# Weight preparation moved behind a norm in the attention, two roots split, and the router's folding moved one stage ahead, on one Trainium2 core

## The chip, the core and the metric

The kernel runs on one core of a Trainium2 chip. Its engines are TensorE (PE, with its weight loads as PEld), VectorE (DVE), ScalarE (ACT), GpSimd (POOL) and SyncE (SP, which only issues DMAs here). The metric is device microseconds of one execution of the whole program. Every engine runs its own list of instructions in order; they wait for one another by semaphores.

## What is computed

A two-layer network on x of 16 batches x 512 tokens x 128 features, float32. Each of four blocks is added to its input after a layer norm:

```
x = x + LN(attention(LN(x)))        # 16 heads of 8, keys and values through a latent of 32
x = x + LN(swiglu(LN(x)))           # hidden 384, weights are int32 times 1/127
x = x + LN(state_space_mlp(LN(x)))  # y = z + scan(rms(z)*scale1); y + gelu(rms(y)*scale2 @ w1 + b1) @ w2 + b2
x = x + LN(experts(LN(x)))          # spikes, router (tanh(cont@rW1+rb1)@rW2), top 2 of 8 experts
```

Here z is LN(x). `rms(z)` divides by sqrt(mean(z*z)+1e-6); a layer norm divides by sqrt(var+1e-5). The state space (16 states per feature) is computed as a convolution: matmuls with taps inside chunks of 128 tokens, and a carry between the four chunks of a batch.

## The kernel before

The program is a row of stages, each an `nc.Block()` with one hand-written list per engine and a barrier at its end: `attention` (tiles a_), `swiglu` (f_), `state_space` (m_), `mlp` (g_), `experts` (e_). X[:, b] is the running sum of batch b, Y[:, b+1] the output of the present block. Nothing schedules; order and semaphores are as written.

**Attention.** One body per batch t. In it 32 turns n: PE makes the scores of two heads against 128 keys (`score`, L629), DVE multiplies a part of them by the decay (`correct`, L775), ACT takes the exponential (L600), PE multiplies by the values (`weighted`, L636). Between the turns other batches' work is laid: POOL splits the next queries and keys into bf16 parts (`lower`), SP stores them to DRAM and reads them back spread by head (`spread_part`), and the norms of batch t-2 are finished: DVE writes `after_var` of t-2 at n = 11 (L179), POOL then inverts it and adds the normed output to X (`add_to`, L218 to L245), DVE waits for that at n = 24 (`wait_added`), takes the statistics of the sum (L165), and POOL inverts those (`next_norm.invert`, into xrstd). The last bodies are t = B-2 and B-1 (`ahead=False`), with B = 16.

After batch B-3's transfers SP also loads the integer weights of the swiglu into the buffers `parts` (L444, L446). POOL's `prepare_next_stage` waits for them, casts them to float (L513, 3 instructions) and normalises batch 0 for the next stage (L101, L104). PE, ACT and DVE need these only after the last body.

**swiglu's end.** `out_statistics`, `normalise` and `statistics` of the last batches run on DVE, then `moments` over all 16 batches at once gives xmean and var. `roots` holds var+1e-5 (for the layer norm) and var*(1+1e-6)+1e-11 (for u, the state space's input, which is normed twice); ACT takes the root of both in one instruction (L1569), DVE two reciprocals (L1712 xrstd, L1713 urstd). Then the barrier.

**state_space.** DVE makes the shifts -mean*rstd for u and for the layer norm (L1891). DVE and ACT then write u, 64 chunks of 128x128: DVE the 36 of batches 0 to 8 (L1895), ACT the 28 of batches 9 to 15 (L1833). PE starts when all of u is there (L1854). ACT then writes the layer norm of batches 0 to 11 into Y (L1839), POOL those of 12 to 15 (L1824, L1826). DVE makes the carries (L1903, L1907, L1909) and lays them in `blocks` (L1914) for PE (L1881), which in between makes the taps' products (L1870).

**mlp's start.** `squares_of` of batch 0, w1 times scale2 (L2078), the router's folding (`fold_router` on PE; `take_turned` and `take_folded` on DVE: s2c_W @ rW1 is put in the place of two matmuls), the first batch's norm (`rms_norm_first`, L2059, L2062), `squares_of` of batch 1, the copy of the transposed batch (`take_T`, L1429), then per batch four matmuls 128x512 (L2039), gelu on ACT, and 16 matmuls back (L2049).

## Time and profile before

| | |
|---|---|
| time, 3 runs | 1303.67 us median (1303.56 to 1304.56) |
| the profiled execution | 1303.26 us, span 1301.4 us, so 1.86 us lie around the span |
| mean granted TensorE clock | 0.962 of 2.4 GHz |
| busy share | PE 90%, DVE 73%, ACT 71%, POOL 50% |
| attention | about 0 to 618 us |
| swiglu | about 620 to 757 us |
| state_space | about 757 to 818 us |
| mlp | about 818 to 951 us |
| experts | to 1301.4 us |

The share of busy time is a mean over stages with different limits. The stage borders are places where all engines stop, so what sets the end differs from stretch to stretch; the rows below come from the stretches around the borders.

### The profile page before, as it was taken

The numbers are of one execution on the slowest core, as the hardware profiler recorded it, in microseconds if no ns is written. First come the engines' busy times: TensorE is split into PE (matmuls) and PEld (weight loads), VectorE is DVE, ScalarE is ACT, GpSimd is POOL, SyncE is SP. The second block draws the span as 40 slices with busy tenths as digits, with TensorE's granted clock in tenths as the row PEclk, the third lists the DMA queues.
The fourth block names the chain that finished last, engine by engine and source line by source line (L and its number), as shares of the span: only waits on it lengthen the run. The fifth ranks groups of instructions, "written<-read, shape, count | busy, mean of one in ns | idle before, by whom it ended". The sixth has DMA issues, their size and how long they took to land. (4 is left out here: it accounts for less than half of the span.)

```text
span 1301.4 us, 27430 instructions
## 1 busy us (share of the span) xinstructions
PE 1169.7 (90%) x7406; PEld 525.2 (40%) x7406; DVE 947.1 (73%) x2956; ACT 928.2 (71%) x1417; POOL 652.3 (50%) x1096
## 2 busy tenths in 40 slices
PE   4889999999999999948899839899979999999994
PEld 1222222322232322213566539577733444444432
DVE  5777777777777777637588877556566888888774
ACT  3979999999999999948556674355445666666664
POOL 5526656665655555334455540224233566666534
PEclk7989999999999999979899969899989999999998
DMA  5664555555555555600970003000000000000001
GB/s 157 143 123 97 106 114 103 110 107 112 108 107 105 108 106 110 118 15 1 228 237 19 1 2 130 1 0 0 1 0 1 10 9 16 16 8 17 9 17 33
DMA packets 71701, 87.97 MB, mean 68 GB/s; under 512 B 10369, under 2 KB 65191, under 8 KB 66023
## 3 DMA queue, kind: packets, MB, share of 16 engines
q1 hardware_dynamic: 69326, 85.81, 30.4%
q10 hardware_dynamic: 2296, 1.25, 0.4%
q8 instruction: 33, 0.54, 0.2%
q14 instruction: 46, 0.37, 0.1%
HBM read 63.84 MB, written 31.59 MB: 73 GB/s over the span
## 5 line engine op out<-in xcount | busy, mean ns | idle before, releaser
L600 ACT ACTIVATE a_probs<-a_S 128x1024 f32<-128x1024 f32 x512 | 492.3, 1035 | 61.0 <-DVE a_S L775 56.3
L775 DVE TENSOR_TENSOR a_S<-a_S,a_tables 128x256 f32<-128x256 f32 (+1 forms) x512 | 279.4, 561 | 129.3 <-PE a_S L629 124.4
L636 PE MATMUL a_O<-a_probs,a_V 128*32 128x512 f32 x2048 | 276.2, 612 | 1.7
L629 PE MATMUL a_S<-a_Qs,a_Ks 48*128 48x512 bf16 x1024 | 182.1, 388 | 34.8 <-ACT a_probs L600 29.3
L629 PEld LDWEIGHTS a_S<-a_Qs,a_Ks 48*128 48x128 bf16 x1024 | 43.6, 93 | 254.2 <-ACT a_probs L600 218.6
L2321 ACT ACTIVATE e_hid<-e_H 128x512 f32<-128x512 f32 x128 | 69.4, 594 | 48.1 <-PE e_H L2429 48.1
L2005 ACT ACTIVATE g_hid<-g_H,w_b 128x512 f32<-128x512 f32 x64 | 43.8, 687 | 57.2 <-PE g_H L2039 57.2
L481 POOL CAST w_first_parts<-a_whole 128x512 bf16<-128x512 f32 x15 | 9.1, 609 | 138.6 <-DVE a_whole L785 138.6
L2427 PE MATMUL e_H<-e_gated,w_We 64*128 64x512 f32 x256 | 73.2, 648 | 1.2 <-ACT e_hid L2321 1.2
L636 PEld LDWEIGHTS a_O<-a_probs,a_V 128*32 128x32 f32 x2048 | 40.4, 108 | 78.8 <-issue 64.8
L2438 PE MATMUL e_O<-e_hid,w_We 128*64 128x512 f32 x256 | 68.7, 609 | 0.4 <-ACT e_hid L2321 0.4
L2039 PE MATMUL g_H<-g_ynT,w_w 128*128 128x512 f32 x128 | 60.7, 619 | 1.6 <-DVE g_ynT L1429 1.6
L2049 PEld LDWEIGHTS g_OUT<-w_w,g_hid 128*128 128x128 f32 x512 | 59.7, 192 | 0.6
L2049 PE MATMUL g_OUT<-w_w,g_hid 128*128 128x128 f32 x512 | 59.7, 275 | 0.0
L2539 DVE TENSOR_TENSOR e_gated<-e_contT,e_G 128x512 f32<-128x512 f32 x64 | 44.0, 687 | 21.2 <-PE e_G L2419 19.7
L1555 ACT ACTIVATE f_gated<-f_G 128x512 f32<-128x512 f32 x48 | 28.6, 596 | 31.2 <-PE f_U L1592 31.2
L1603 PE MATMUL f_OUT<-w_wT,f_hid 128*128 128x128 f32 x384 | 46.5, 278 | 1.0 <-DVE XY L1669 1.0
L1603 PEld LDWEIGHTS f_OUT<-w_wT,f_hid 128*128 128x128 f32 x384 | 44.2, 192 | 5.5 <-DVE XY L1669 4.3
L652 PE MATMUL a_M<-ident,a_Osb 128*128 128x128 f32 x256 | 42.1, 287 | 4.6 <-DVE a_whole L785 3.8
L1638 DVE SCALAR_TENSOR_TENSOR f_hid<-f_U,f_gated 128x512 f32<-128x512 f32 x48 | 33.0, 690 | 14.6 <-ACT f_gated L1555 14.6
L218 POOL TENSOR_TENSOR g_power_rstd<-g_power_var,g_power_half 128x4 f32<-128x4 f32 (+1 forms) x15 | 15.1, 1007 | 56.2 <-DVE g_power_var L195 55.9
L652 PEld LDWEIGHTS a_M<-ident,a_Osb 128*128 128x128 f32 x256 | 27.1, 141 | 39.7 <-issue 26.4
(431 smaller groups left out, 2466.9 us busy)
## 6 DMA issues: line engine op xcount, KB each, us to landing
a_parts_dram<-a_parts SPq DMA_DIRECT2D x62, 192.0 KB, 5.7
a_Qs<-a_parts_dram SPq DMA_DIRECT2D x60, 192.0 KB
m_taps_by_step<-h_taps SPq DMA_DIRECT2D x8, 1024.0 KB, 13.6
m_taps<-m_taps_by_step SPq DMA_DIRECT2D x8, 1024.0 KB, 5.1
a_Qs<-a_parts_dram SPq DMA_DIRECT2D x60, 128.0 KB
a_parts_dram<-w_first_parts SPq DMA_DIRECT2D x32, 192.0 KB, 2.7
a_Ks<-a_parts_dram SPq DMA_DIRECT2D x30, 192.0 KB
a_Qs<-a_parts_dram SPq DMA_DIRECT2D x68, 64.0 KB
```

The costliest lines, as they stand in the source:

```text
L600: act.activation(probs[n % KEPT][:], S[n % RING][:], ACT.Exp).then_inc(exped, 1)
L629: mm = pe.matmul(S[n % RING][:, par, :], Ks[p][rows, pr, kb * P:(kb + 1) * P], Qs[p][Q_OF(kb)][rows, pr, :], start=True, stop=True)
L636: mm = pe.matmul(O[VC * j:VC * (j + 1), :], V[q][:, kb, HG * g + j, :], probs[(2 * m + j // 2) % KEPT][:, j % 2, :], start=(kb == 0), stop ...
L652: mm = pe.transpose(M[:, tile_of(core, c)], src[:, tile_of(core, c)], core.ident[:])
L775: v.tensor_tensor(s[:, :, where], s[:, :, where], wide, ALU.mult).then_inc(corrected, 1)
L1603: mm = pe.matmul(OUT[q].t[:, tile_of(core, c)], hid[q][:, m, tile_of(core, c)], wT[2][:, m, :], start=(m == 0), stop=(m == FC - 1))
L2039: pe.matmul(H[m][:], w1[:, tile_of(core, m)], ynT[p][:], start=True, stop=True).then_inc(h_full, 1)
L2049: mm = pe.matmul(o, hid[p][:, m, tile_of(core, c)], w2[:, m, :], start=False, stop=(m == FC - 1), skip_group_check=True)
L2321: HB[h].emptied(act.activation(hid[:, 2 * k + h], HB[h].t[:], ACT.Relu))
L2427: pe.matmul(HB[h].t[:], W.We1[half[h], k], gated[k % 2][half[h]], start=True, stop=False)
L2438: mm = pe.matmul(OB.t[h * M:(h + 1) * M], W.We2[:, 2 * k + h, :], hid[:, 2 * k + h, :], start=(k == 0 and h == 1), stop=(k == PAIRS - 1), ...
L2539: GB.emptied(v.tensor_tensor(gated[k % 2][:], contT[q][:], GB.t[:], ALU.mult))
```

## The change

Five edits.

1. In the attention POOL's `prepare_next_stage()` no longer stands at the head of body B-2 but at its end, behind `add_to` and `next_norm.invert` of batch B-4.
2. At swiglu's end the two roots have tensors of their own (xrstd is used in place): ACT takes u's root first, then the layer norm's; DVE there makes only the reciprocal of u's. The other reciprocal and its shift go into state_space, behind DVE's chunks of u. DVE now writes 38 chunks of u, ACT 26. ACT and POOL wait for the late shift (`UPPER`) before they write the layer norm.
3. The router's folding goes from mlp's start to swiglu's end: `fold_router` on PE behind the last `down`, into swiglu's PSUM tile G[0]; `take_turned`, `take_folded` and the cast of `select` (was DVE's L1086 in `shape_biases`) on ACT.
4. w1 times scale2 goes from DVE at mlp's start to POOL at the end of its list in state_space, as a `tensor_tensor` 128x512.
5. At mlp's start DVE takes the statistics of batch 1 between the variance of batch 0 and its norm, and the copy of the transposed batch 0 comes behind only the short rest of `squares_of` of batch 1.

```diff
@@ attention, POOL
             def body(t, p, first=False, ahead=True, more=True, fresh=True):
-                if isinstance(t, int) and t == B - 2:
-                    prepare_next_stage()
                 if not isinstance(t, int) or t >= 2:
                     out_norm.add_to(pool, t - 2, p)
                 if not ahead:
...
                     next_norm.invert(pool, t - 2, core.xrstd, p)
                     if not more:
                         next_norm.invert(pool, t - 1, core.xrstd, 1 - p)
+                    else:
+                        prepare_next_stage()
                     return
@@ Weights
+    def take_selection(self, act):
+        act.wait_ge(*self.experts)
+        act.activation(self.select.rearrange("p k m -> p (k m)"), self.table[:, 0:self.select.shape[1] * P], ACT.Copy).then_inc(self.shaped, 1)
+
-    def take_turned(self, v, ps):
-        v.wait_ge(self.folded, self.TURNED)
-        v.tensor_copy(self.s2cT, ps[0:self.s2cT.shape[0], 0:self.s2cT.shape[1]]).then_inc(self.folded, 1)
+    def take_turned(self, act, ps):
+        act.wait_ge(self.shaped, self.SELECTED)
+        act.wait_ge(self.folded, self.TURNED)
+        act.activation(self.s2cT, ps[0:self.s2cT.shape[0], 0:self.s2cT.shape[1]], ACT.Copy).then_inc(self.folded, 1)
@@ swiglu, ACT, PE, DVE
+            OUT[1].read(act, B // 2)
+            W.take_selection(act)
+            W.take_turned(act, G[0])
+            W.take_folded(act, G[0])
             act.wait_ge(steps, ROOTS)
-            act.activation(roots[:], roots[:], ACT.Sqrt).then_inc(rooted, 1)
+            act.activation(uroots[:], uroots[:], ACT.Sqrt).then_inc(rooted, 1)
+            act.activation(xroots, xroots, ACT.Sqrt).then_inc(rooted, 1)
...
             down(1, B // 2)
+            W.fold_router(core, pe, G[0])
...
             v.wait_ge(rooted, 2)
-            tick.mark(v.reciprocal(core.xrstd[:, 0:B], roots[:, 0]))
-            tick.step(v.reciprocal(core.urstd[:, 0:B], roots[:, 1]))
+            tick.step(v.reciprocal(core.urstd[:, 0:B], uroots[:]))
@@ state_space
-    ACT_U, ACT_BATCHES = 7, 12
+    DVE_CHUNKS, ACT_BATCHES = 38, 12
...
+            pool.wait_ge(dve_ready, UPPER)
             for b in range(ACT_BATCHES, B):
...
+            pool.wait_ge(*W.mlp)
+            pool.tensor_tensor(W.w1[:], W.w1[:], W.scale2[:].to_broadcast(list(W.w1.shape)), ALU.mult)
...
+            act.wait_ge(dve_ready, UPPER)
             act.preload_act_table(ACT.Exp)
...
+            shift_by(ushift, core.urstd)
+            for b, c in chunks[:DVE_CHUNKS]:
...
+            v.reciprocal(core.xrstd[:, 0:B], core.xrstd[:, 0:B]).then_inc(dve_ready, 1)
+            v.wait_ge(dve_ready, UPPER_ROOTS)
+            shift_by(shift, core.xrstd)
@@ mlp
-            W.fold_router(core, pe, folding)
-            pe.wait_ge(scaled, 1)
...
             power.squares_of(v, 0, Y[:, 1])
-            v.wait_ge(*W.mlp)
-            v.tensor_scalar(w1[:], w1[:], s2[:], None, ALU.mult).then_inc(scaled, 1)
-            W.take_turned(v, folding)
+            power.moments_of(v, 1, Y[:, 2], only_stats=True)
             rms_norm_first()
-            W.take_folded(v, folding)
-            power.squares_of(v, 1, Y[:, 2])
+            power.squares_of(v, 1)
             take_T(0, 0)
```

The order of POOL's list at body B-2 of the attention, before (line numbers of the changed kernel are one higher here; after_ and next_ are the two norms' tiles):

```order
L513 CAST a_whole<-w_first_parts 128x384
L513 CAST a_whole<-a_parts 128x384 x2
L101 TENSOR_TENSOR a_xn<-XY,xmean 128x512
L104 TENSOR_TENSOR a_xn<-a_xn,xrstd 128x512
L218 TENSOR_TENSOR after_rstd<-after_var,next_half 128x4
L220 TENSOR_TENSOR after_work<-after_rstd 128x4
L222 TENSOR_TENSOR after_work<-after_work,after_var 128x4
L224 TENSOR_TENSOR after_work<-next_three,after_work 128x4
L226 TENSOR_TENSOR after_rstd<-after_rstd,after_work 128x4
L241 TENSOR_TENSOR XY<-XY,after_neg 128x512
L243 TENSOR_TENSOR XY<-XY,after_rstd 128x512
L245 TENSOR_TENSOR XY<-XY 128x512
```

and in the changed kernel:

```order
L225 TENSOR_TENSOR after_work<-next_three,after_work 128x4
L227 TENSOR_TENSOR after_rstd<-after_rstd,after_work 128x4
L242 TENSOR_TENSOR XY<-XY,after_neg 128x512
L244 TENSOR_TENSOR XY<-XY,after_rstd 128x512
L246 TENSOR_TENSOR XY<-XY 128x512
L219 TENSOR_TENSOR xrstd<-next_var,next_half 128x4
L221 TENSOR_TENSOR next_work<-xrstd 128x4
L223 TENSOR_TENSOR next_work<-next_work,next_var 128x4
L225 TENSOR_TENSOR next_work<-next_three,next_work 128x4
L227 TENSOR_TENSOR xrstd<-xrstd,next_work 128x4
L514 CAST a_whole<-w_first_parts 128x384
L514 CAST a_whole<-a_parts 128x384 x2
```

The three casts, which wait for the integer weights, stood ahead of the `add_to` of batch B-4 and now stand behind it and behind the inversion of its sum.

The order of ACT's list across the border between swiglu and state_space, before:

```order
L1565 ACT_TABLE_LOAD
L1567 ACTIVATE f_out_work<-f_out_var 128x4
L1569 ACTIVATE f_roots<-f_roots 128x128
L1438 UNCONDITIONAL_BRANCH
L1828 UNCONDITIONAL_BRANCH
L1833 ACTIVATE m_u<-XY,in_rstd,urstd 128x128 x28
L1836 ACT_TABLE_LOAD
L1839 ACTIVATE XY<-XY,in_mean,xrstd 128x128 x48
```

and in the changed kernel (w_table is the router's table, w_rb its bias):

```order
L1574 ACTIVATE f_out_work<-f_out_var 128x4
L1124 ACTIVATE w_wT<-w_table 128x512
L1130 ACTIVATE w_table<-f_G 64x256
L1136 ACTIVATE w_rb<-f_G,w_rb 64x1
L1137 ACTIVATE w_table<-f_G 128x128
L1580 ACTIVATE f_uroots<-f_uroots 128x64
L1581 ACTIVATE xrstd<-xrstd 128x64
L1445 UNCONDITIONAL_BRANCH
L1844 UNCONDITIONAL_BRANCH
L1848 ACTIVATE m_u<-XY,in_rstd,urstd 128x128 x26
L1852 ACT_TABLE_LOAD
L1855 ACTIVATE XY<-XY,in_mean,xrstd 128x128 x48
```

The root of 128x128 became two of 128x64 with four folding instructions ahead of them, and no table load came in between.

The order of DVE's list at mlp's start, from behind the variance of batch 0 to the copy of the transposed batch 0, before:

```order
L1123 COPY w_table<-g_fold 64x256
L2059 RECIPROCAL g_power_rstd<-g_power_work 128x4
L2062 TENSOR_SCALAR g_yn<-XY,g_power_rstd 128x128 x4
L1129 TENSOR_TENSOR w_rb<-g_fold,w_rb 64x1
L1130 COPY w_table<-g_fold 128x128
L186 BN_STATS yst<-XY 128x6 x4
L189 SCALAR_TENSOR_TENSOR g_power_diff<-yst 128x4
L190 SCALAR_TENSOR_TENSOR g_power_square<-yst 128x4
L191 SCALAR_TENSOR_TENSOR g_power_spread<-yst 128x4
L193 TENSOR_TENSOR g_power_square<-g_power_diff,g_power_square 128x4
L195 SCALAR_TENSOR_TENSOR g_power_var<-g_power_spread,g_power_square 128x4
L1429 COPY g_ynT<-g_TP 128x512
```

and in the changed kernel:

```order
L165 BN_STATS yst<-XY 128x6 x4
L2076 RECIPROCAL g_power_rstd<-g_power_work 128x4
L2079 TENSOR_SCALAR g_yn<-XY,g_power_rstd 128x128 x4
L190 SCALAR_TENSOR_TENSOR g_power_diff<-yst 128x4
L191 SCALAR_TENSOR_TENSOR g_power_square<-yst 128x4
L192 SCALAR_TENSOR_TENSOR g_power_spread<-yst 128x4
L194 TENSOR_TENSOR g_power_square<-g_power_diff,g_power_square 128x4
L196 SCALAR_TENSOR_TENSOR g_power_var<-g_power_spread,g_power_square 128x4
L1436 COPY g_ynT<-g_TP 128x512
```

The scaling of w1, which stood just ahead of the first of these rows, and the three instructions of the folding are gone, and the statistics of batch 1 (L165) stand ahead of the norm of batch 0 (L2079), so that only five short instructions are left between that norm and the copy (L1436).

## Rows read from the trace of the kernel before

**Rows 1.** The page, part 1: busy time, share of the span, instructions, by engine
```profile
PE 1169.7 (90%) x7406; PEld 525.2 (40%) x7406; DVE 947.1 (73%) x2956; ACT 928.2 (71%) x1417; POOL 652.3 (50%) x1096
```

**Rows 2.** Timeline of POOL, 530 to 575 us: start, length, instruction, count, [idle, releaser]
```profile
555.84 0.50 POOL L513 CAST a_whole<-w_first_parts 128x384 f32<-128x384 int32 x1 [22.18 <-DMA a_parts<-L_ffn_w_down]
...
559.42 1.01 POOL L218 TENSOR_TENSOR after_rstd<-after_var,next_half 128x4 f32<-128x4 f32 x1
...
564.54 1.26 POOL L245 TENSOR_TENSOR XY<-XY 128x512 f32<-128x512 f32 x1 [0.18 <-POOL XY L243]
```

**Rows 3.** Timeline of DVE, 530 to 615 us
```profile
538.25 0.16 DVE L179 SCALAR_TENSOR_TENSOR after_var<-after_spread,after_square 128x4 f32<-128x4 f32 x1
...
565.84 0.87 DVE L165 BATCH_NORM_STATS2 xst<-XY 128x6 f32<-128x128 f32 x4 [15.29 <-POOL XY L245]
...
567.37 1.62 DVE L775 TENSOR_TENSOR a_S<-a_S,a_tables 128x256 f32<-128x256 f32 x3
...
575.43 0.43 DVE L775 TENSOR_TENSOR a_S<-a_S,a_tables 128x256 f32<-128x256 f32 x1 [2.44 <-PE a_S L629]
...
603.01 1.02 DVE L775 TENSOR_TENSOR a_S<-a_S,a_tables 128x256 f32<-128x256 f32 x2
...
609.21 0.43 DVE L775 TENSOR_TENSOR a_S<-a_S,a_tables 128x256 f32<-128x256 f32 x1 [1.47 <-PE a_S L629]
```

**Rows 4.** Timeline of ACT, 560 to 580 us
```profile
567.83 1.02 ACT L600 ACTIVATE a_probs<-a_S 128x1024 f32<-128x1024 f32 x1 [15.54 <-DVE a_S L775]
...
572.70 1.94 ACT L600 ACTIVATE a_probs<-a_S 128x1024 f32<-128x1024 f32 x2 [0.61 <-DVE a_S L775]
...
575.90 3.00 ACT L600 ACTIVATE a_probs<-a_S 128x1024 f32<-128x1024 f32 x3 [1.26 <-DVE a_S L775]
```

**Rows 5.** Stretch 570 to 575 us: PE, PEld, DVE, ACT, POOL busy; PEclk; DMA
```profile
570.00:575.00 5.00, 5.00 (x24) 1.02 (x17) 1.29 (x3) 4.03 (x5) 0.16 (x1) 0.53 0.00 0
```

**Rows 6.** Waits of the DMA queue's engine, 480 to 620 us: total, times, longest
```profile
SPq L452 <- DMA a_Ks<-a_parts_dram: 4.8, 1, 4.8
```

**Rows 7.** Timeline of SP's queue, 540 to 550 us
```profile
548.96 0.48 SPq L446 DMA_DIRECT2D a_parts<-L_ffn_w_down  x1
```

**Rows 8.** Timeline of ACT, DVE and PE, 755 to 770 us
```profile
755.51 0.31 ACT L1569 ACTIVATE f_roots<-f_roots 128x128 f32<-128x128 f32 x1 [6.62 <-DVE f_roots L1709]
...
755.85 0.55 DVE L1712 RECIPROCAL xrstd<-f_roots 128x64 f32<-128x64 f32 x1 [0.38 <-ACT f_roots L1569]
...
757.35 0.23 DVE L1891 SCALAR_TENSOR_TENSOR in_rstd<-xmean,urstd 128x64 f32<-128x64 f32 x1 [0.54 <-PEq L1438]
...
757.63 9.32 DVE L1895 TENSOR_SCALAR m_u<-XY,xmean,urstd 128x128 f32<-128x128 f32 x36
...
757.75 10.88 ACT L1833 ACTIVATE m_u<-XY,in_rstd,urstd 128x128 f32<-128x128 f32 x28 [1.93 <-DVE in_mean L1891]
...
768.78 8.08 PE L1854 MATMUL m_bank<-m_u,m_falls 128*32 128x48 f32 x256 [25.36 <-ACT m_u L1833]
```

**Rows 9.** Timeline of POOL and DVE, 592 to 594 us
```profile
592.79 1.04 POOL L243 TENSOR_TENSOR XY<-XY,after_rstd 128x512 f32<-128x512 f32 x1 [0.18 <-POOL XY L241]
...
592.82 1.02 DVE L177 TENSOR_TENSOR after_square<-after_diff 128x4 f32<-128x4 f32 x1
```

**Rows 10.** Timeline of POOL and PE, 781 to 785 us
```profile
781.12 1.49 POOL L1826 TENSOR_TENSOR XY<-XY,xrstd 128x512 f32<-128x512 f32 x1
...
784.88 2.87 PE L1881 MATMUL m_bank<-m_blocks,m_rises 128*128 128x192 f32 x16 [0.70 <-DVE m_blocks L1914]
```

**Rows 11.** Timeline of DVE and PE, 821 to 839 us
```profile
823.89 0.68 DVE L1429 COPY g_ynT<-g_TP 128x512 f32<-128x512 f32 x1
...
821.99 1.11 PE L1410 MATMUL g_TP<-ident,g_yn 128*128 128x128 f32 x4
...
824.70 6.25 PE L2039 MATMUL g_H<-g_ynT,w_w 128*128 128x512 f32 x7 [1.59 <-DVE g_ynT L1429]
...
835.44 3.60 PE L2039 MATMUL g_H<-g_ynT,w_w 128*128 128x512 f32 x8
```

More of the change, by code:

```diff
@@ L179, in moments_of, with squares_of @@
         v.scalar_tensor_tensor(self.var4[:, k], spread, 4.0 / D, square, ALU.mult, ALU.add).then_inc(self.steps, 1)
-    def squares_of(self, v, u, src):
+    def squares_of(self, v, u, src=None):
         at = lambda n: u * self.MEASURE + (self.start + n)
         st, diff, spread, square = self.st[:, u], self.diff[:, u], self.spread[:, u], self.square[:, u]
-        for c in range(self.core.NT):
-            op = v.bn_stats(st[:, c], src[:, c])
-        op.then_inc(self.steps, 1)
+        if src is not None:
+            for c in range(self.core.NT):
+                op = v.bn_stats(st[:, c], src[:, c])
+            op.then_inc(self.steps, 1)
         v.wait_ge(self.steps, at(1))
@@ L1083, in shape_biases @@
         rest = picked = scratch[:, 0:HH + M + 2 * D]
-        step = Tally(v, self.shaped)
+        step = Tally(v, self.shaped, start=self.SELECTED)
         v.wait_ge(*self.experts)
-        step.mark(v.tensor_copy(self.select.rearrange("p k m -> p (k m)"), self.table[:, 0:PAIRS * P]))
+        v.wait_ge(self.shaped, self.SELECTED)
         step.step(v.tensor_copy(part[0], self.biases[:]))
@@ L1103, in shape_biases @@
         step.settle()
-        assert step.n == self.SHAPED
+        assert step.start + step.n == self.SHAPED
     TURNED, TAKEN, FOLDED, MERGED = range(1, 5)
@@ L1452, in swiglu @@
         mean, var = (sb(n, [P, B, NT]) for n in ("mean", "var"))
-        roots = sb("roots", [P, 2, B, NT])
+        uroots, xroots = sb("uroots", [P, B, NT]), core.xrstd[:, 0:B]
         out = Norm(core, ctx, "f_out", core.yst[:, 1:B + 1], affine=False)
@@ L1707, in _ @@
             moments(v, tick, core.xst[:], core.xmean[:, 0:B], var[:], mean[:])
-            tick.mark(v.tensor_scalar(roots[:, 0], var[:], 1e-5, None, ALU.add))
-            tick.mark(v.tensor_scalar(roots[:, 1], var[:], 1.0 + 1e-6, 1e-11, ALU.mult, ALU.add))
+            tick.mark(v.tensor_scalar(xroots, var[:], 1e-5, None, ALU.add))
+            tick.mark(v.tensor_scalar(uroots[:], var[:], 1.0 + 1e-6, 1e-11, ALU.mult, ALU.add))
             assert tick.n == ROOTS
             v.wait_ge(rooted, 2)
-            tick.mark(v.reciprocal(core.xrstd[:, 0:B], roots[:, 0]))
-            tick.step(v.reciprocal(core.urstd[:, 0:B], roots[:, 1]))
+            tick.step(v.reciprocal(core.urstd[:, 0:B], uroots[:]))
 class Taps:
@@ L1802, in state_space @@
         ACT_UPPER, ACT_A = 1, 2
-        SHIFT, U = 2, 3
+        SHIFT, U, UPPER_ROOTS, UPPER = 1, 2, 3, 4
+        chunks = [(b, c) for b in range(B) for c in range(NT)]
         ends_full, states, blocks_done = sem("ends_full"), sem("states"), sem("blocks_done")
@@ L1830, in _ @@
             act.wait_ge(dve_ready, SHIFT)
-            for b in range(B - ACT_U, B):
-                for c in range(NT):
-                    op = act.activation(u[:, b, c], X[:, b, c], ACT.Identity, bias=ushift[:, b, c:c + 1],
-                                        scale=core.urstd[:, b, c:c + 1])
+            for b, c in chunks[DVE_CHUNKS:]:
+                op = act.activation(u[:, b, c], X[:, b, c], ACT.Identity, bias=ushift[:, b, c:c + 1],
+                                    scale=core.urstd[:, b, c:c + 1])
             op.then_inc(act_ready, 1)
+            act.wait_ge(dve_ready, UPPER)
             act.preload_act_table(ACT.Exp)
@@ L1889, in _, with shift_by @@
             tick = Tally(v, states, start=GROUPS // LANES)
-            for dst, by in ((ushift, core.urstd), (shift, core.xrstd)):
+            def shift_by(dst, by):
                 v.scalar_tensor_tensor(dst[:], core.xmean[:, 0:B], -1.0, by[:, 0:B], ALU.mult, ALU.mult)\
                  .then_inc(dve_ready, 1)
-            for b in range(B - ACT_U):
-                for c in range(NT):
-                    op = v.tensor_scalar(u[:, b, c], X[:, b, c], core.xmean[:, b, c:c + 1], core.urstd[:, b, c:c + 1],
-                                         ALU.subtract, ALU.mult)
+            shift_by(ushift, core.urstd)
+            for b, c in chunks[:DVE_CHUNKS]:
+                op = v.tensor_scalar(u[:, b, c], X[:, b, c], core.xmean[:, b, c:c + 1], core.urstd[:, b, c:c + 1],
+                                     ALU.subtract, ALU.mult)
             op.then_inc(dve_ready, 1)
+            v.reciprocal(core.xrstd[:, 0:B], core.xrstd[:, 0:B]).then_inc(dve_ready, 1)
+            v.wait_ge(dve_ready, UPPER_ROOTS)
+            shift_by(shift, core.xrstd)
             by_chunk = state[:].rearrange("p g (b c) -> p g b c", c=CARRY)
@@ L1951, in mlp @@
         H = [ctx.enter_context(nc.psum_tensor(f"g_H{k}", [P, 512], F32)) for k in range(FC)]
-        folding = ctx.enter_context(nc.psum_tensor("g_fold", [P, 512], F32))
         OUT = [Bank(core, ctx, f"g_OUT{p}") for p in range(2)]
```

14 lines of the change are left out of this document (7 added, 7 removed).

## The prediction

> **What bounds the kernel now.** I read the page first: TensorE is busy for 90% of the span [rows 1]. Where PE is full, work taken off the others brings nothing, so I looked for where PE stands still, by the list of stretches, and then at each engine's timeline there. Three places are touched by the change.
>
> The first is inside the attention. From 550.55 to 565.84 DVE stands for 15.29 us and waits for POOL's sum in X (its n = 24, `wait_added`) [rows 3]; ACT stands for 15.54 us behind it [rows 4], and PE with them. POOL is late because it stood for 22.18 us ahead of the first cast, until the integer weights had landed at 555.8; only then came the casts and the norm of batch 0 (3.58 us, 555.84 to 559.42) and the inversion with the addition (559.42 to 565.80, 6.38 us) [rows 2]. The last weight's DMA was issued only at 548.96 [rows 7]. So all engines wait for data that nobody needs before the end of the stage. When they go on, PE's clock is at half: 0.53 granted in 570 to 575, with PE busy for the whole stretch [rows 5].
>
> The second is the border between swiglu and state_space: PE is idle for 25.36 us and starts at 768.78, when ACT's 28 chunks of u are there (757.75 + 10.88 = 768.63). DVE ends its 36 at 766.95 [rows 8]. The third is mlp's start: the transposes of batch 0 end at 823.10, but DVE copies them from 823.89 only, since the statistics of batch 1 stand between, and PE starts the first wide matmul at 824.70 after 1.59 us of idleness [rows 11].
>
> **Step 1: prepare behind the addition.** What released POOL's addition is `after_var`, written at 538.41 [rows 3]. In the changed order POOL is free then (its idle time goes back to 533.66 [rows 2]) and needs 6.38 us, so X is summed at 544.8. DVE asks for it at 550.55: 5.7 us to spare. The stall goes as a whole: **15.3 us**. The casts then wait for the same landing at 555.84 with nothing queued behind them but the addition of batch B-3, which in the kernel before DVE asks for at about 603.01 - 1.53 = 601.5 (1.53 is the way from the statistics to the next `correct`, 565.84 to 567.37) [rows 3].
>
> The clock: from turn 25 to turn 31 the stalled batch needs 575.43 - 567.37 = 8.06 us, the next one, at full clock, 609.21 - 603.01 = 6.20 [rows 3]. ACT, which sets the pace, shows the same: it waits 0.61 + 1.26 = 1.87 us within these turns [rows 4]. Without the stall PE never falls to half, and this comes back. Bounds: 0, if ACT would have lost the time in the next turns anyway, and 1.9. I take **1.8**, since both engines' rows give nearly the same.
>
> Is the next batch's input there so early? SP waited 4.8 us for the last keys after its last issue [rows 6, 7], so they landed between 554 and 555. Batch B-1's first scores come at the earliest just ahead of 575.9 - 17.1 = 558.8 [rows 4]. Some 4 us are left.
>
> **Step 2: roots and chunks.** The root of both in one takes 0.31 us [rows 8]; half of it is a little shorter, say 0.05. One reciprocal of 0.55 leaves the path, in the pipelined row about 0.5. One shift less ahead of the chunks is 0.14 (757.35 to 757.63 hold two) [rows 8]. ACT's start moves from 757.75 to about 757.08. A chunk costs ACT 10.88/28 = 0.389 and DVE 9.32/36 = 0.259 [rows 8]. ACT: 757.08 + 26 x 0.389 = 767.18. DVE: 756.96 + 38 x 0.259 = 766.80. PE starts 0.15 after the later: 767.33 for 768.78, **1.45 us** earlier. The late reciprocal and shift (0.55 + 0.23) end on DVE at about 767.6, ahead of its next work, which waits for PE's first 64 matmuls; ACT has its table load and the layer norm after that, earlier than before.
>
> The folding costs nothing: ACT waits 6.62 us for the variance [rows 8]. It gets four instructions, each not above the 0.31 to 0.69 us of rows of such width [rows 8, 11], and between them PE has five small matmuls, bounded by two groups of transposes at 1.11 [rows 11]: together below 4.5 us. If that cover were gone, it would be up to 4.5. The order of ACT's list shows that no table load comes in.
>
> **Step 3: w1 on POOL, and a shared port.** POOL has been at work until 782.61; the multiplication is one more instruction of 1.0 to 1.5 us [rows 2, 9, 10], and POOL is not asked for anything until the stage's end at 818. But DVE makes and lays the carries at the same time, and PE waits for them by 0.70 us already [rows 10]; in the changed kernel they fall 1.45 earlier, into POOL's work. What such a meeting costs is in the trace: a DVE instruction on 4 columns took 1.02 us, from 592.82 to 593.84, while POOL's L243 ran from 592.79 to 593.83 [rows 9]; DVE's neighbours of that size take 0.16 [rows 3]. So the bound is between 0 and one such block, 1.5. I take **-0.4**, nearer to nothing, because PE's idle time is only 0.70 now although POOL is at work until 2.3 us ahead of 784.88.
>
> The Trainium skill ("SBUF — State Buffer", section "Who interferes with whom") says that a Vector instruction with two SBUF inputs contends with a GpSimd instruction that reads SBUF, and that the shared pair is held for a whole instruction; the 1.02 us beside POOL's 1.04 agree with it. By this rule alone each carry would pay, and the step would give nothing; that is the second rival.
>
> **Step 4: mlp's start.** Ahead of the norm of batch 0 the scaling and one copy go and the statistics of batch 1 come: about even. The transposes no longer wait for the folding's matmuls; I take 0.2 of that (bounds: 0 and one group of four, 1.11). Behind them DVE is free: 823.89 - 823.10 = 0.79 [rows 11]. Together **1.0 us**. The clock is at half here with and without the change (6.25 us for 7 matmuls against 3.60 for 8 later) [rows 11], and it rises during PE's first batch. If it rose a whole such batch earlier or later, that would be some 3 us; I expect less than 1 either way, as PE's work moves as one.
>
> Everything after is PE's own pace, so these gains reach the end.
>
> **Sum.** 15.3 + 1.8 + 1.45 - 0.4 + 1.0 = 19.15. Made against the profiled execution: 1303.26 - 19.15 = 1284.1. The median of the runs is 0.41 above that execution, so I forecast **1284.5 us**.
>
> **Rivals.**
> 1. *The clock gives nothing back.* ACT is the pace and would catch up in the next batch: 1.8 less, 1286.3. Against it stand ACT's gaps, which are within the slow stretch.
> 2. *The port eats step 2.* DVE's carries are blocked by POOL's last norms and by w1: 1.05 more is lost, 1285.6. For it: rows 9. Against: the PE idle time now is only 0.70 with POOL at work.
> 3. *The keys come too late.* PE now asks for batch B-1's keys at 558.8 instead of 575. Each us by which they land after that costs one; with 562 it is 3.2, 1287.7.
> 4. *The stall stays, by another releaser.* If POOL could not start the addition at 538.4, or DVE's wait hung on the preparation still, only steps 2 to 4 would be left: 2.05, 1301.6, within 0.2%.
> 5. *The wait moves to batch B-1 and grows: slower.* POOL's casts now stand ahead of the addition of batch B-3. DVE asks for that at 601.5 - 17.1 = 584.4; casts, norm and addition take 3.58 + 6.38, so a landing after 574.4 costs. It makes the kernel slower from 574.4 + 19.2 = 593.6 on; at 600 the time is 1303.67 + 6.4 = 1310. The landing now is 555.8, and nothing ahead of it in SP's queue moves.
>
> **Chances.** Forecast 0.78, rival 1 0.07, rival 2 0.08, rival 3 0.03, rival 4 0.02, rival 5 0.02. The range has as its lower end the forecast less 0.1 (clock at its bound), 0.4 (no port), 0.9 (all of the transposes' wait) and about 1 for an earlier rise of the clock: 1282.1. The upper end takes in rivals 1 and 2 and a later rise of the clock by 0.4: 1287.8 holds rival 3 too. A measurement of this kernel can tell 0.2%, 2.6 us, from no change. Faster than that: 0.96; within: 0.02; slower: 0.02.
>
> **What would show it.** Step 1: DVE's statistics of batch B-4 (L165) follow turn 24 with no idle time; POOL's 22 us idle stretch shrinks to a wait of little over 1 us ahead of the casts, behind the inversion; the granted clock stays at 1.00 until the stage's end; the stage ends 17 us earlier. Step 2: PE's first matmul of the stage (L1854) starts some 11.5 us behind the start of DVE's first reciprocal, where it was 768.78 - 755.85 = 12.9, with ACT's 26 chunks as its releaser, and the folding lies on ACT ahead of the roots. Step 3: PE's idle time ahead of the first carry product (now 0.70) says whether the port cost 0, 0.4 or 1.5. Step 4: the copy of batch 0 begins within 0.1 us of the transposes' end. Wrong would be: an idle stretch of PE between 553 and 585, or one ahead of batch B-1's first scores with a DMA as releaser.

## The result

The changed kernel takes 1288.74 us in the median of four runs (1287.9 to 1289.76), the kernel before 1304.12 us beside it (1303.56 to 1306.04): a ratio of 0.988, 95% interval 0.9863 to 0.9897. It is faster, by 15.4 us. I had forecast 1284.5 us, with a range of 1282.1 to 1287.8; the time lies 0.9 us outside, and some 4 us of the forecast gain did not come. The section on the profile goes by the profiled run, 1287.9 us with a span of 1285.9.

### The profile page after: what moved, and what is told of

It is laid out like the page before. It is cut to its first block and busy times, and to the rows that moved or that the text cites. A ratio compares the mean times of both kernels' runs of the same rounds, so it can differ in the third digit from the quotient of the medians.

```text
span 1285.9 us, 27394 instructions
## 1 busy us (share of the span) xinstructions
PE 1168.2 (91%) x7367; PEld 527.1 (41%) x7406; DVE 948.0 (74%) x2953; ACT 928.8 (72%) x1420; POOL 655.1 (51%) x1097
## 5 line engine op out<-in xcount | busy, mean ns | idle before, releaser
L2553 DVE TENSOR_TENSOR e_gated<-e_contT,e_G 128x512 f32<-128x512 f32 x64 | 44.0, 687 | 21.1 <-PE e_G L2433 17.8
L2266 POOL TENSOR_TENSOR XY<-XY (+1 forms) x28 | 35.2, 1271 | 17.3 <-ACT XY L2313 17.3
L653 PEld LDWEIGHTS a_M<-ident,a_Osb 128*128 128x128 f32 x256 | 26.8, 140 | 38.9 <-issue 25.5
```

The costliest lines, as they stand in the source:

```text
L653: mm = pe.transpose(M[:, tile_of(core, c)], src[:, tile_of(core, c)], core.ident[:])
L2553: GB.emptied(v.tensor_tensor(gated[k % 2][:], contT[q][:], GB.t[:], ALU.mult))
```

## The profile after

The page, part 1 of the changed kernel; beside [rows 1] nothing has moved by more than a share point or two.

```profile
PE 1168.2 (91%) x7367; PEld 527.1 (41%) x7406; DVE 948.0 (74%) x2953; ACT 928.8 (72%) x1420; POOL 655.1 (51%) x1097
```

**The attention.** The timeline of POOL and then that of DVE in body B-2 of the changed kernel (start, length, instruction, idle time and its releaser):

```profile
540.34 1.01 POOL L219 TENSOR_TENSOR after_rstd<-after_var,next_half 128x4 f32<-128x4 f32 x1 [4.93 <-DVE after_var L179]
...
545.48 1.28 POOL L246 TENSOR_TENSOR XY<-XY 128x512 f32<-128x512 f32 x1 [0.18 <-POOL XY L244]
553.98 1.02 POOL L219 TENSOR_TENSOR xrstd<-next_var,next_half 128x4 f32<-128x4 f32 x1 [7.22 <-DVE next_var L179]
...
556.74 0.50 POOL L514 CAST a_whole<-w_first_parts 128x384 f32<-128x384 int32 x1 [0.23 <-POOL xrstd L227]
```

```profile
551.86 0.42 DVE L776 TENSOR_TENSOR a_S<-a_S,a_tables 128x256 f32<-128x256 f32 x1
552.19 0.86 DVE L165 BATCH_NORM_STATS2 xst<-XY 128x6 f32<-128x128 f32 x4
...
553.71 1.02 DVE L776 TENSOR_TENSOR a_S<-a_S,a_tables 128x256 f32<-128x256 f32 x2
```

The sum in X is there at 546.76, DVE asks for it at 552.2 and goes on without idle time. The 15.29 us of [rows 3] and the 22.18 us of [rows 2] are gone. The casts wait 0.23 us. PE stays at full clock:

```profile
553.00:558.00 5.00, 3.96 (x32) 0.91 (x34) 3.73 (x11) 4.86 (x7) 3.08 (x8) 1.00 0.56 116
```

(the stretch, PE, PEld, DVE, ACT, POOL busy, granted clock, DMA share, GB/s). But the same point, the end of turn 24, comes at 552.28, where it came at 550.55 in the profile of before: 1.7 us had been lost earlier, in code that is the same in both kernels. No wait of PE for the keys of batch B-1 appears behind it.

**The border to state_space.** DVE's reciprocal starts at 740.60 and PE's first matmul at 752.21, 11.6 us behind it for 11.5 forecast (12.9 before [rows 8]). ACT's 26 chunks end 0.14 us ahead of it; the profile names DVE's late reciprocal (L1915) as releaser, but PE needs of that semaphore only the count that stands at DVE's last chunk, one step earlier:

```profile
741.95 10.12 ACT L1848 ACTIVATE m_u<-XY,in_rstd,urstd 128x128 f32<-128x128 f32 x26 [1.24 <-DVE in_rstd L1907]
...
752.21 8.13 PE L1870 MATMUL m_bank<-m_u,m_falls 128*32 128x48 f32 x256 [16.12 <-DVE xrstd L1915]
```

The folding lies on ACT ahead of the roots and costs nothing:

```profile
733.60 0.61 ACT L1124 ACTIVATE w_wT<-w_table 128x512 bf16<-128x512 f32 x1
...
736.28 0.26 ACT L1137 ACTIVATE w_table<-f_G 128x128 f32<-128x128 f32 x1
740.32 0.26 ACT L1580 ACTIVATE f_uroots<-f_uroots 128x64 f32<-128x64 f32 x1 [3.77 <-DVE f_uroots L1722]
```

Behind it the gain is lost again. DVE, PE and POOL of the changed kernel, from their timelines:

```profile
760.99 0.90 DVE L1927 TENSOR_TENSOR m_faded<-m_state,h_fade 128x512 f32<-128x512 f32 x1
761.92 1.59 DVE L1929 TENSOR_TENSOR m_state<-m_state,m_faded 128x512 f32<-128x512 f32 x1
763.55 1.47 DVE L1927 TENSOR_TENSOR m_faded<-m_state,h_fade 128x512 f32<-128x512 f32 x1
765.05 1.57 DVE L1929 TENSOR_TENSOR m_state<-m_state,m_faded 128x512 f32<-128x512 f32 x1
766.66 4.34 DVE L1934 COPY m_blocks<-m_state 32x384 f32<-32x384 f32 x8
...
760.27 7.40 PE L1886 MATMUL m_bank<-m_u,m_taps 128*128 128x64 f32 x64
769.57 2.87 PE L1897 MATMUL m_bank<-m_blocks,m_rises 128*128 128x192 f32 x16 [1.90 <-DVE m_blocks L1934]
...
765.97 1.49 POOL L1840 TENSOR_TENSOR XY<-XY,xrstd 128x512 f32<-128x512 f32 x1
767.42 1.15 POOL L1842 TENSOR_TENSOR w_w<-w_w,w_scale 128x512 f32<-128x512 f32 x1
```

The same instructions of DVE in the kernel before:

```profile
777.50 1.09 DVE L1907 TENSOR_TENSOR m_faded<-m_state,h_fade 128x512 f32<-128x512 f32 x1
778.63 1.58 DVE L1909 TENSOR_TENSOR m_state<-m_state,m_faded 128x512 f32<-128x512 f32 x1
780.24 1.50 DVE L1907 TENSOR_TENSOR m_faded<-m_state,h_fade 128x512 f32<-128x512 f32 x1
781.77 1.57 DVE L1909 TENSOR_TENSOR m_state<-m_state,m_faded 128x512 f32<-128x512 f32 x1
783.38 2.92 DVE L1914 COPY m_blocks<-m_state 32x384 f32<-32x384 f32 x8
```

PE now waits 1.90 us for the carries, where it waited 0.70 [rows 10]. From the reciprocal to the end of PE's last matmul of the stage it is 61.13 us, and 61.14 in before.

**mlp's start.** The copy of the transposed batch starts at 807.60, 0.04 us behind the transposes' end, and PE's first wide matmul comes 1.0 us earlier in its stage:

```profile
807.60 0.69 DVE L1436 COPY g_ynT<-g_TP 128x512 f32<-128x512 f32 x1 [0.59 <-PE g_TP L1417]
...
806.44 1.12 PE L1417 MATMUL g_TP<-ident,g_yn 128*128 128x128 f32 x4 [4.71 <-DVE g_yn L2079]
808.42 5.53 PE L2056 MATMUL g_H<-g_ynT,w_w 128*128 128x512 f32 x8 [0.86 <-DVE g_ynT L1436]
```

From there on the kernels are the same, and yet it takes 1285.92 - 808.42 = 477.5 us to the end of the span, where before took 1301.4 - 824.70 = 476.7 (start in [rows 11]).

## The experiments

Since three stretches differ in code that no edit touched, every profile is read by the same marks: ACT's 65th exponential of the attention, swiglu's first matmul, DVE's reciprocal, PE's last matmul of state_space, PE's first wide matmul of mlp, the end. The table behind the experiments has them.

**1. The changed kernel again.** 

> The changed kernel, nothing edited, profiled and timed again. Question: are the parts that came out worse than predicted properties of the kernel, or of one execution? Theory A (execution): the granted clock at the start of the attention rose 5.3 us later in the profiled execution of the changed kernel than in that of before (48.5 for 43.2 on the trace's own clock), and the half clock around the border from mlp to the experts held 13.7 us for 6.8; both are chance, so in another profile the end of turn 24 of body B-2 may come anywhere from 550.5 to 552.3 and the stretch from the second wide batch of mlp to the end of the span may take 465.9 to 467.9 us; the median over the runs is then 1287 to 1289. Theory B (kernel): both stretches repeat within 0.3 us, 552.3 and 467.9, and the median is 1288.7.

Measured: 1289.13 us (1288.3 to 1289.86), ratio 0.9877 (0.9845 to 0.991). Turn 24 ended at 552.71; from mlp's wide matmul to the end it took 479.0 for 477.5. Both theories have a miss: turn 24 lies 0.4 us behind the latest that they gave, and the stretch behind mlp's start is longer than either allowed. The median is theory B's. So the losses are not one odd execution.

**2. Edit 1 alone.** 

> Before with edit 1 alone (the preparation of the next stage moved behind the addition and the inversion in body B-2). By step 1 as predicted: 15.3 + 1.8 = 17.1 us less, 1287.0. By the trace of the changed kernel: 16.9 us less locally, and if the later rise of the clock at the start is chance of one execution, 1287.2 in the median. Rival: the gain is given back in part by a clock at half later in the program, whose phase has moved: then 1288 to 1290, with the swiglu and the later stages longer than before's in the profile.

```diff
-                if isinstance(t, int) and t == B - 2:
-                    prepare_next_stage()
...
+                    else:
+                        prepare_next_stage()
```

Measured: 1287.91 us (1283.97 to 1289.97), ratio 0.986 (0.9831 to 0.9889). This edit alone is worth as much as all five. Its profile has the changed kernel's 494.9 us from the 65th exponential to swiglu, before's 61.1 and 7.6 for the two stretches behind the reciprocal, and 477.2 from there to the end.

**3. Edits 2 to 5 alone.** 

> The changed kernel with edit 1 undone (edits 2 to 5 alone). As predicted, steps 2 to 4 give 2.05 us: 1303.67 - 2.05 = 1301.6. By the stages of the changed kernel's trace: swiglu -0.4, state_space +0.4, mlp's start -2.2, so 1301.4 if the 1.9 us that were lost around the border from mlp to the experts are chance of one execution. Rival: this loss belongs to edits 2 to 5 (the clock at mlp's start moves the clock's later stretches at half): then 1303.4, no change, with half clock of 13 us or more around that border again. PE's idle time ahead of the first carry product should be about 1.9 us here as in the changed kernel (0.70 before) if the port is its cause.

The edit is that of experiment 2 taken back in the changed kernel. Measured: 1304.15 us beside 1303.44, ratio 0.9995 (0.9978 to 1.0012): no change, as the rival said. But the interval reaches from 2.9 us faster to 1.6 slower, so it holds the 2.05 us that I gave these four edits too, and the times alone don't decide. The profile does: from the reciprocal to state_space's last matmul 60.9 us, to mlp's first wide matmul 6.7 (1.0 gained), and then 478.9 to the end, so that the gained microsecond is lost again. PE's idle time ahead of the first carry product is 1.87 us.

**4. w1 on ACT.** 

> The changed kernel with the scaling of w1 by scale2 on ScalarE at swiglu's end (in the 3.8 us in which it waits for the variance) and not on GpSimd in state_space. Theory 1 (the w1 multiplication on GpSimd blocks VectorE's carries): DVE's copies into blocks take 2.9 us for 8 again, not 4.3, PE's idle time ahead of the first carry product falls from 1.90 to 0.7 or less, and the kernel is 1.2 us faster than the changed one, 1287.5. Theory 2 (it is GpSimd's last norm of 1.49 us that blocks them, since the carries now fall 1.45 us earlier; w1 only comes behind): PE still waits 1.3 to 1.9 us and the time moves by under 0.5, 1288.3 to 1288.7.

```diff
-            pool.wait_ge(*W.mlp)
-            pool.tensor_tensor(W.w1[:], W.w1[:], W.scale2[:].to_broadcast(list(W.w1.shape)), ALU.mult)
...
             W.take_folded(act, G[0])
+            act.wait_ge(*W.mlp)
+            act.activation(W.w1[:], W.w1[:], ACT.Identity, scale=W.scale2[:])
```

Measured: 1287.98 us (1286.03 to 1290.8), ratio 0.9878 (0.985 to 0.9906). The time doesn't tell it from the changed kernel; the trace does (DVE, PE):

```profile
763.92 1.58 DVE L1929 TENSOR_TENSOR m_state<-m_state,m_faded 128x512 f32<-128x512 f32 x1
765.53 3.58 DVE L1934 COPY m_blocks<-m_state 32x384 f32<-32x384 f32 x8
...
767.69 2.87 PE L1897 MATMUL m_bank<-m_blocks,m_rises 128*128 128x192 f32 x16 [1.14 <-DVE m_blocks L1934]
```

The first carry product comes 28.15 us behind the reciprocal, for 28.97 and 28.80: 0.7 to 0.8 us of the loss is w1. The rest is in the carry instructions, of which three still take 1.5 to 1.6 us beside POOL's norms. That lies between the two theories: PE waits 1.14 us, where they gave 0.7 or less and 1.3 to 1.9.

**5. POOL's last norms late (the late kernel, below).** 

> The changed kernel, where GpSimd waits for VectorE's first two layings of the carries (blocks_done 2) ahead of its last two batches of the layer norm and of w1, so that VectorE's carries run with GpSimd quiet. Theory (GpSimd's 128x512 instructions stretch VectorE's four carry instructions, 1.5 to 1.6 us each, and the eight copies, 4.3): the carry instructions take about 0.9 each, the copies 2.9, PE's first carry product follows its taps without idle time, 27.1 us behind DVE's reciprocal of u's root where it is 28.8 to 29.0 in the changed kernel, and the kernel is 1.8 us faster than the changed one, about 1287.0, if VectorE's first addition to Y (which waits for GpSimd's last norm, then at about 771 us) is not late. Rival 1: the carry instructions take 1.5 us by themselves; then nothing moves but the order, 1288.7. Rival 2: the addition to Y comes late and holds PE's banks; then PE stands ahead of the third set of taps instead, and the gain is gone.

```diff
                 pool.tensor_tensor(Y[:, b + 1], Y[:, b + 1], wide(core.xrstd, b), ALU.mult).then_inc(pool_a, 1)
+                if b == ACT_BATCHES + 1:
+                    pool.wait_ge(blocks_done, 2)
             pool.wait_ge(*W.mlp)
```

Measured: 1284.59 us (1283.66 to 1284.77), ratio 0.9851 (0.9834 to 0.9867). DVE, PE and POOL of this kernel:

```profile
759.82 0.87 DVE L1929 TENSOR_TENSOR m_faded<-m_state,h_fade 128x512 f32<-128x512 f32 x1
760.73 0.89 DVE L1931 TENSOR_TENSOR m_state<-m_state,m_faded 128x512 f32<-128x512 f32 x1
761.66 0.87 DVE L1929 TENSOR_TENSOR m_faded<-m_state,h_fade 128x512 f32<-128x512 f32 x1
762.56 0.90 DVE L1931 TENSOR_TENSOR m_state<-m_state,m_faded 128x512 f32<-128x512 f32 x1
763.50 2.93 DVE L1936 COPY m_blocks<-m_state 32x384 f32<-32x384 f32 x8
...
766.32 2.80 PE L1899 MATMUL m_bank<-m_blocks,m_rises 128*128 128x192 f32 x16
...
766.51 1.24 POOL L1838 TENSOR_TENSOR XY<-XY,xmean 128x512 f32<-128x512 f32 x1 [6.94 <-DVE m_blocks L1936]
```

The wait of 6.94 us ahead of POOL's norm is the edit's. With POOL quiet the four instructions take 0.87 to 0.90 us for up to 1.59, PE has no idle time, and the carry product comes at 26.67, 2.1 to 2.3 us earlier than in the changed kernel. The theory holds for the carries and the rivals fall; the time fell by more than the 1.8 us expected, since the stretch behind mlp's start came out shorter too (476.6 us, in the table). DVE pays part of it back later, off the path (a `shape_biases` instruction of 0.62 takes 1.34 beside the late norms).

**6. Edit 2 alone.** 

> Before with edit 2 alone (roots split, 38 and 26 chunks, late reciprocal and shift; w1 and the folding as before). One look at the stage's marks, counted from DVE's first reciprocal behind the roots: PE's first matmul at 11.6 us for 12.9, as in the changed kernel. Theory 1 (w1 on GpSimd eats the gain): the first carry product then comes at 27.9 to 28.2 for 29.0 before, as with w1 on ScalarE. Theory 2 (edit 2 is eaten by the norms of GpSimd alone): 28.8 to 29.0.

Measured: 1304.29 us in one run. The marks: PE's start at 11.60, the first carry product at 27.68. So edit 2 by itself carries 1.35 of its 1.45 us to that point against the first profile of before, and 0.85 against the fourth, in which the product came at 28.53. Theory 1 had 27.9 to 28.2, theory 2 28.8 to 29.0; this is nearer to theory 1, in one profile (PE):

```profile
783.93 2.87 PE L1883 MATMUL m_bank<-m_blocks,m_rises 128*128 128x192 f32 x16 [0.92 <-DVE m_blocks L1920]
```

It is less than the 28.15 of experiment 4, which has no w1 on POOL either. There POOL's norms lay about 1.4 us later behind the reciprocal than here (its last ended at 26.8 for 25.4) and reached into the copies. Where they lie differs between executions with the length of POOL's two fills of `blocks` ahead of them, 4.22 us here, the shortest of all profiles, and 4.99 in experiment 4.

**7, 8. Before again, twice.** 

> The kernel before, nothing edited, profiled again. Is its first profile typical in three places where code common to both kernels gave other times in other executions? Theory (executions differ): turn 64 of the attention comes at 109.0 to 113.1 us as the wait for the second body's keys falls out (3.7 to 8.2 us seen); the first 16 wide matmuls of mlp take 16.9 rather than 18.4 us; PE's first 300 instructions of the experts take 75.8 to 77.1 rather than 72.9, with 10 us of half clock around the border instead of 3.4. Rival (they belong to the kernel): 18.4 and 72.9 are seen again.

 

> The kernel before once more, for the same three places: with three profiles of before and one of the attention edit alone (which has the same code from the swiglu on), it is told how often the stretch of 72.9 us comes and how far turn 64 moves. Expected by the theory that executions differ: at most one of them like the first.

Measured: 1313.22 and 1305.1 us. The profile of experiment 8, the third of this kernel, is like the first behind mlp's start (476.6 us to the end). That of experiment 7, the second (479.4), is not, and it shows something else: the granted clock fell within state_space (0.50 in the 5 us from the first carry product), and the stage took 66.3 us for 61.1. What differs ahead of that is on POOL and DVE (timelines of the second profile):

```profile
769.65 6.02 POOL L1821 MEMSET m_blocks<- 128x1536 f32 x2 [9.58 <-DVE m_u L1895]
774.63 3.79 POOL L1824 TENSOR_TENSOR XY<-XY,xmean 128x512 f32<-128x512 f32 x1
...
774.16 2.03 DVE L1903 TENSOR_TENSOR m_state<-m_bank,h_coef 128x384 f32<-128x384 f32 x1 [4.57 <-PE m_bank L1854]
...
786.82 4.35 DVE L1914 COPY m_blocks<-m_state 32x384 f32<-32x384 f32 x8
```

The fills start as far behind the reciprocal as in the first profile (11.15 us) but last 6.02 us for 5.32. DVE's instruction on PE's sums (L1903), 0.56 us when the fills are over, takes 2.03 beside them, and POOL's norms come so late that they reach into the copies (4.35 us for 2.92). PE idled 1.91 us ahead of the carry product, and its clock went to half.

**9 to 12. A delay ahead of mlp.** 

> The changed kernel with five spare 128x128 instructions of VectorE (about 1.0 us) ahead of the first norm of mlp, so that all of mlp and the experts start about 1 us later. Question: where do the clock's half stretches behind that point fall, and is that set by the kernel? In ten profiles the time from mlp's first wide matmul to the end of the span took 476.6 (three, first kernel twice and the one with late norms; the experts' first 300 instructions of PE 72.9), 477.2 to 477.5 (three) or 479.0 to 479.4 us (four). Theory 1 (the kernel's own timing sets it; the start of mlp 1.0 us earlier is what moved the changed kernel from 476.6 to 477.5 and more): with the delay it is 476.6 again, 350 behind the experts' start, and the median is the changed kernel's plus 1.0 minus 0.9 to 2.4: 1287.4 to 1288.9, not slower. Theory 2 (it falls by chance in each execution): the time is that of the changed kernel plus 1.0, 1289.8, and the stretch may be any of the three.

 

> The kernel with GpSimd's norms late (measured 1284.6) with the same 1.0 us ahead of mlp's first norm. Theory 1 (set by the kernel's timing): it leaves the good place, the stretch from mlp's first wide matmul takes 477.2 to 479.4 us, and the median is 1284.6 + 1.0 + 0.6 to 2.8 = 1286.2 to 1288.4: one microsecond of waiting costs more than one. Theory 2 (chance): 1285.6.

 

> The same with ten spare instructions, about 2.0 us. Theory 1: the stretch takes 477.2 to 479.4 us too, so that 1287.2 to 1289.4 are measured, or, if it comes to the better of the two bad places, little more than with 1 us. Theory 2: 1286.6.

 

> The kernel with GpSimd's norms late, nothing edited, once more. Theory 1 (the kernel's timing sets the clock's places behind mlp's start): 476.6 us from mlp's first wide matmul and 349.7 from the experts' start again, 1284.6 in the median. Theory 2 (chance): 477.2 to 479.4 for that stretch in this profile is as likely, and the median over the runs is 1284.6 to 1286.5.

```diff
+                for c in range(DELAY):
+                    v.tensor_scalar(spare[:, c], Y[:, 1, c % NT], rstd[:, 0, 0:1], None, ALU.mult)
                 for c in range(NT):
                     op = v.tensor_scalar(yn[:, c], Y[:, 1, c], rstd[:, 0, c:c + 1], None, ALU.mult)
```

(DELAY is 5 for 1 us and 10 for 2.) Measured: experiment 9, 1291.04 us (1289.58 to 1292.07), ratio 0.99 (0.9885 to 0.9915), 477.5 us to the end; 10, 1286.2 (1284.03 to 1287.96), 0.9871 (0.9855 to 0.9886), 476.3; 11, 1287.43 (1285.96 to 1289.52), 0.9881 (0.9864 to 0.9897), 477.6; 12, 1283.78 (1282.81 to 1286.0), 0.9852 (0.9839 to 0.9866), 476.6. Theory 1 has two misses: a delay of 1 us neither brought the changed kernel back to 476.6 nor took the late kernel away from it. Two came out as it said: 2 us did take the late kernel away, and without a delay it repeated its place. Theory 2, chance, allows each of these stretches; its medians were off by 0.6 to 1.2 us in all four. Experiment 9 met long fills as experiment 7 did, besides (PE, POOL):

```profile
750.12 8.03 POOL L1834 MEMSET m_blocks<- 128x1536 f32 x2 [9.96 <-DVE m_u L1912]
...
770.44 4.85 PE L1897 MATMUL m_bank<-m_blocks,m_rises 128*128 128x192 f32 x14 [3.40 <-DVE m_blocks L1934]
```

**13 to 16. Two more profiles of each kernel.** 

> The changed kernel, nothing edited. Theory 1 (the kernel's own timing sets where the clock's half stretches fall behind mlp's start): from mlp's first wide matmul to the end of the span 477.5 or 479.0 us again. Theory 2 (chance): 476.6 is as likely as in before.

 

> The changed kernel once more, the same question: 477.5 to 479.0 by theory 1, 476.6 about as often as in before by theory 2.

 

> The kernel before, nothing edited. Theory 1: 476.6 us from mlp's first wide matmul to the end, as in its first and third profile. Theory 2: anything of 476.6 to 479.4.

 

> The kernel before once more, the same question: 476.6 by theory 1.

Measured: changed, 1290.58 and 1289.03 us; before, 1301.39 and 1307.36. From mlp's first wide matmul to the end the changed kernel took 479.4 and 477.5 us and before 476.6 twice, as theory 1 said but for 0.4 us.

The marks of all profiles of the two kernels, in us, each the difference of two rows of the timelines:

| | before, five profiles | changed, four profiles |
|---|---|---|
| start to the 65th exponential | 109.0, 112.0, 110.8, 108.3, 112.6 | 110.7, 111.2, 110.7, 110.0 |
| to swiglu's first matmul | 511.5, 511.3, 511.8, 511.4, 510.2 | 494.9, 494.9, 494.7, 494.7 |
| swiglu, to the reciprocal | 135.3, 135.3, 135.3, 134.9, 134.5 | 135.0, 135.0, 134.4, 134.4 |
| to state_space's last matmul | 61.1, 66.3, 61.0, 60.7, 63.9 | 61.1, 61.0, 62.6, 63.8 |
| to mlp's first wide matmul | 7.7, 7.2, 7.7, 7.7, 7.7 | 6.7, 6.7, 6.7, 6.7 |
| to the end of the span | 476.7, 479.4, 476.6, 476.6, 476.6 | 477.5, 479.0, 479.4, 477.5 |
| span | 1301.4, 1311.4, 1303.2, 1299.5, 1305.5 | 1285.9, 1287.7, 1288.6, 1287.0 |

The late kernel has 58.8 in the fourth row in each of four profiles (two of them with the delay behind it), and in the sixth 476.6 twice without the delay, 476.3 and 477.6 with it. The other kernels have in the sixth row: edit 1 alone 477.2, edits 2 to 5 alone 478.9, w1 on ACT 477.5, edit 2 alone 479.2, the changed kernel with the delay 477.5.

## Why the prediction was wrong

**Step 1, the stall and the clock: right.** From the 65th exponential to swiglu it is 16.4 us less in the mean of the profiles, for 17.1 forecast: the whole of the stall, and 1.1 of the 1.8 us for the clock. Turns 25 to 31 do take 6.20 us as forecast, and PE's clock stays at 1.00 up to 600 us, but the last body gives some back: its first 16 turns take 17.88 us, where four of five profiles of before have 17.66, and from there to swiglu it is 26.3 for 26.1 in the mean. Rivals 1, 3, 4 and 5 are out.

**Step 2: right up to PE's start** (1.32 us for 1.45), and the folding was hidden.

**Step 3 is a term that was mis-sized: 0.4 forecast, about 1.3 measured.** In the profiles whose clock did not fall in this stage PE starts 1.3 us earlier behind the reciprocal, and its last matmul ends no earlier: 61.1 and 61.0 us, for 61.1, 61.0 and 60.7 in before. The second rival had the mechanism, and with 1.05 us more about its price; by itself it would have given 1285.6 us, so it does not account for the whole miss. I had argued that the port costs little because PE idled only 0.70 us in before though POOL was at work. What I didn't see is that before was already paying: three of its carry instructions took 1.58, 1.50 and 1.57 us, and experiment 5 shows what they take alone, 0.87 to 0.90. A short wait behind stretched work is no evidence that the stretching is cheap. My bound of one block of 1.5 us had no ground either, since several instructions in a row are stretched. The edit then moved the carries 1.3 us towards POOL's norms, which did not move themselves (POOL's last norm starts 25.4 us behind the reciprocal, 25.3 in before, since POOL waits for DVE's chunks of u, of which there are two more), and put w1 behind them. Experiment 4 gives w1 0.7 to 0.8 of the loss, experiment 5 all of it and 0.9 us more. How the rest splits between the nearer norms and the length of the fills is not shown: experiment 6, with the norms as near and no w1 on POOL, kept 0.85 to 1.35 us, with the shortest fills of all.

The Trainium skill ("SBUF — State Buffer", section "Who interferes with whom") has a Vector instruction with two SBUF inputs contend with GpSimd's reads, and the one that comes second wait for the whole instruction of the other. That the carry instructions take 1.58 for 0.89 us agrees with the contention; the 0.69 us more is less than one of POOL's norm instructions, which take 1.04 us at their shortest and 1.49 to 1.61 beside the carries, so both sides pay. The copies have one input and are not what that sentence speaks of; their 4.34 for 2.93 us is a measurement of its own.

**Step 4: right**, 1.03 us for 1.0.

**"Everything after is PE's own pace, so these gains reach the end" is the step that failed otherwise.** From mlp's first wide matmul on, where I expected less than 1 us either way, the changed kernel takes 0.8 to 2.8 us more than four of the five profiles of before, 1.6 between the medians. Where it goes is seen in the granted clock at the experts' start (before from 956.7, changed from 939.3, both 5 us behind PE's first matmul of the stage; columns as above):

```profile
956.70:966.70 10.00, 6.66 (x24) 3.20 (x26) 8.73 (x31) 4.14 (x9) 3.95 (x7) 0.83 0.00 0
966.70:976.70 10.00, 7.38 (x40) 3.08 (x36) 6.84 (x23) 3.87 (x9) 2.21 (x6) 0.83 0.00 1
```

```profile
939.30:949.30 10.00, 7.08 (x20) 3.34 (x22) 8.79 (x31) 4.16 (x9) 3.98 (x7) 0.63 0.00 0
949.30:959.30 10.00, 7.17 (x32) 2.89 (x29) 5.73 (x17) 1.94 (x4) 1.82 (x5) 0.69 0.00 0
```

The two levels are 1.2 and 2.4 GHz, 0.5 and 1.0 granted. PE is busy for about as long in both; in the changed kernel the clock is at half for longer (0.63 and 0.69 granted for 0.83 twice), and PE gets 20 + 32 instructions done for 24 + 40. In return the time from mlp's first wide matmul to the 17th is shorter (17.2 to 17.8 us for 18.4 in four of five profiles of before), but by less. The late kernel looks like before (profile of experiment 5):

```profile
937.00:947.00 10.00, 6.66 (x24) 3.21 (x26) 8.74 (x31) 4.14 (x9) 3.97 (x7) 0.83 0.00 0
```

So the code is the same and the clock isn't. In all 18 profiles the stretch goes with the clock at its start: where the first 10 us from mlp's first wide matmul were granted 0.69 to 0.75, it took 476.3 to 476.7 us (seven profiles), where they were granted 0.76 to 0.85, 477.2 to 479.4 (eleven). In these profiles a clock that was higher there was followed by more time at half at the experts' border (0.61 to 0.71 granted in the two windows shown above, for 0.83).

What decides between the two was not settled. The kernel's own timing seems to have a part in it: with before's code from the swiglu on, four of six profiles have the short stretch (experiment 2 is the sixth), with the changed kernel's code none of seven (its four, experiments 3, 4 and, with the delay, 9), with the norms late three of four. Experiments 13 to 16, two profiles of each kernel on one chip, say the same: 479.4 and 477.5 for 476.6 twice. Against a theory of the instant of arrival alone stand experiment 2, which reached mlp as late in its stage as before and got 477.2, and the delays of experiments 9 and 10.

**The sum.** 16.4 + 0.3 (swiglu) + 0 (state_space) + 1.0 - 1.6 = 16.1 us, and the medians of the spans differ by 1303.2 - 1287.4 = 15.8. (The 0 of state_space is that of the profiles in which the clock did not fall there; it fell in two of the five and in two of the four.) Forecast were 19.15. Of the 3.1 us between, 0.7 are step 1's, 1.05 steps 2 and 3 together, and 1.6 the clock behind mlp's start, less the 0.3 of the swiglu, which I had not booked. Steps 2 to 4 give 1.0 + 0.3 - 1.6, about nothing, and experiment 3, which has them alone, shows no change either, within its interval.

**The version that beats both** is that of experiments 5 and 12: 1284.6 and 1283.8 us, nine runs from 1282.8 to 1286.0, where ten of the changed kernel lie between 1287.9 and 1290.6. Its 4 to 5 us are 2.2 to 5.0 in state_space, which always took 58.8, and 0.9 to 2.8 of clock behind it. The two kernels never ran beside each other; against before beside each they are 0.985 twice and 0.988 twice.

## What to carry to other kernels

Before a move is priced by an idle time of today, compare the durations of the same instruction form with and without the neighbour at work; what is already stretched hides the price. A stall of all engines in a stage where nobody needs the data is worth its whole length, and is the first thing to look for. Gains of about 1 us ahead of a stage border should not be booked before the border's clock has been seen in several profiles: mlp's start gained 1.0 us in every profile of the changed kernel, and the stretch behind it took more than that back in the medians.
